# Maximum units in pairs on two row halves of TensorE, and the first expert of a second MoE ahead of its routing weights

## The reference

```python
# latent attention: 16 heads, 64 latent features, 1444 context positions a batch row
q_r = jnp.einsum('bshq,hqr->bhsr', q_big, W_qr)
k_r = jnp.einsum('bld,hdr->bhlr', kv_r, W_kr)
scores = jnp.einsum('bhsr,bhlr->bhsl', q_r, k_r)
attn = jax.nn.softmax(scores, axis=-1)
ctx_c = jnp.einsum('bhsl,bld->bhsd', attn, kv_r)
# second MoE: 32 experts, 8 of them a token, inner size 128, and a shared expert
router_scores = jax.nn.sigmoid(t @ Wr)
_, idx = jax.lax.top_k(router_scores + expert_bias[None, :], TOPK)
w = jnp.take_along_axis(router_scores, idx, axis=1)
w = w / jnp.sum(w, axis=-1, keepdims=True)
act = jax.nn.silu(g) * u
moe = jnp.einsum('tei,te,eih->th', act, wfull, Wd)
```

## Time and profile before

| what | us |
|---|---|
| median of 3 runs (1599.54 to 1603.27) | 1599.77 |
| the profiled execution's own time | 1590.53 |
| its span, first to last instruction | 1588.8 |
| PE busy / DVE / POOL / ACT | 1470.2 / 899.7 / 781.4 / 620.0 |
| latent attention: first to last reduction of a unit | 474.3 to 922.6 |
| first hidden product of the second MoE | 1359.69 |

### The profile page before, as it was taken

How to read it: one execution, slowest core, us unless ns; L and a number is a source line. 1 busy time by engine, 2 the same in 40 slices (tenths; PEclk the granted TensorE clock), 3 DMA queues, 4 the chain that set the end, 5 groups by cost and what they waited for, 6 DMA issues and landing times. The chain is left out here.

```text
span 1588.8 us, 20773 instructions
## 1 busy us (share of the span) xinstructions
PE 1470.2 (93%) x7316; PEld 1102.4 (69%) x7316; DVE 899.7 (57%) x1581; ACT 620.0 (39%) x1117; POOL 781.4 (49%) x605
## 2 busy tenths in 40 slices
PE   7898999899978999999999998978999998799998
PEld 4586565544445766766766665567988877799998
DVE  1573111255556676786776763567878774444444
ACT  2243121133341344344343342356666653333333
POOL 0760102135544897797797764057465541233332
PEclk7798999699997999999999999789999998899999
DMA  8004111611001010110110000200110001343441
GB/s 301 1 1 146 51 47 38 212 48 49 1 11 55 29 57 4 54 57 1 57 57 1 19 1 2 81 27 10 46 54 2 27 1 41 105 122 121 121 121 51
DMA packets 60317, 88.61 MB, mean 56 GB/s; under 512 B 7556, under 2 KB 44612, under 8 KB 60230
## 3 DMA queue, kind: packets, MB, share of 16 engines
q1 hardware_dynamic: 59206, 85.82, 16.9%
q0 software_dynamic: 1024, 1.64, 0.4%
HBM read 81.92 MB, written 5.41 MB: 55 GB/s over the span
## 5 line engine op out<-in xcount | busy, mean ns | idle before, releaser
L965 ACT ACTIVATE prob<-PS 121x800 f32<-121x800 f32 x192 | 158.3, 838 | 248.8 <-PE PS L1937 246.0
L1344 DVE TENSOR_REDUCE mx<-PS 128x1 f32<-128x482 f32 (+1 forms) x312 | 185.6, 649 | 44.7 <-PE PS L1917 43.5
L618 POOL TENSOR_TENSOR e_wl<-e_wf,e_wh 128x768 fp32r<-128x768 f32 x33 | 70.8, 2144 | 181.0 <-ACT e_wh L883 159.1
L695 POOL TENSOR_TENSOR hT<-hT,prob 121x800 f32<-121x800 f32 x56 | 109.3, 1951 | 66.4 <-ACT prob L965 64.3
L1916 PE MATMUL PS<-kth,qs 128*128 128x482 f32 (+1 forms) x312 | 128.6, 412 | 13.4 <-DVE kl L1337 5.8
L1952 PE MATMUL PS<-prob,kvn 121*64 121x400 f32 (+1 forms) x768 | 136.1, 503 | 0.9 <-ACT prob L965 0.9
L695 POOL TENSOR_TENSOR xc<-xc,prob 121x800 f32<-121x800 f32 x56 | 117.7, 2101 | 13.6 <-ACT prob L965 8.3
L1917 PE MATMUL PS<-kl,qm 66*128 66x482 f32 (+1 forms) x312 | 122.5, 393 | 0.0
L1934 PE MATMUL PS<-qs,kth 128*121 128x400 f32 (+1 forms) x384 | 111.6, 373 | 7.8 <-DMA qm<-nml 4.8
L1937 PE MATMUL PS<-qm,kl 66*121 66x400 f32 (+1 forms) x384 | 103.8, 352 | 0.0
L1952 PEld LDWEIGHTS PS<-prob,kvn 121*64 121x64 f32 (+1 forms) x768 | 52.3, 137 | 71.2 <-issue 68.6
(11 more groups left out here) (278 smaller groups left out, 3565.9 us busy)
## 6 DMA issues: line engine op xcount, KB each, us to landing
e_wb<-routing SPq DMA_DIRECT2D x32, 400.0 KB, 3.9
wgu<-in_L_ffn_gate_up_proj SPq DMA_DIRECT2D x8, 1024.0 KB, 14.0
krt<-in_ctx_T SPq DMA_DIRECT2D x8, 722.0 KB, 4.1
ksw<-in_ctx_Tswap SPq DMA_DIRECT2D x8, 722.0 KB, 5.7
wdn<-in_L_ffn_down_proj SPq DMA_DIRECT2D x8, 512.0 KB, 7.9
wq<-in_L_ffn_Wq SPq DMA_DIRECT2D x4, 1024.0 KB, 5.1
wo<-in_L_ffn_Wo SPq DMA_DIRECT2D x4, 1024.0 KB, 5.5
e_wf<-in_L_ffn_Wg SPq DMA_DIRECT2D x32, 128.0 KB, 2.2
```

What stands on the lines that cost most here:

```text
L618: pool.tensor_tensor(m["wl"][:, slot], m["wf"][:, slot], m["wh"][:, slot].bitcast(fp32), ALU.subtract).then_inc(ms["wlo"], 1)
L695: pool.tensor_tensor(acc, acc, prob[:, n % RING], ALU.add).then_inc(xb["ap"], 1)
L965: act.activation(prob[0:k, n % RING], PS[0:k, 2 * (n % 2):2 * (n % 2) + 2, 0:GC], ACT.Exp).then_inc(xb["ex"], 1)
L1344: dve.tensor_reduce(mx3[:, m, g:g + 1], PS[:, 4 + k % 3, 0:SEG[g][1]], AX.X, ALU.max).then_inc(xb["free"], 1)
```

## The change

In the latent attention a unit's second product has 64 rows. Units are issued in pairs: both high products, then both low ones, the first unit's on partitions 0 to 63 and the second's on 64 to 127, where `kl2` and `qm2` now have a second copy. The ones in rows 64 and 65 of `kl2` are written after a batch row's units, once per row; the scores keep their 66 rows. `UNITS` has mostly even steps, and in steps 8 and 14 the last two units are issued behind `values`. In the second MoE the barrier RT1 is gone, TensorE issues the first expert's hidden products ahead of the transposes of the routing weights, and the waits are moved to the places that need the data. The diff, cut to its core:

```diff
-        UNITS = (0, 0, 0, 0, 2, 4, 6, 8, 11, 14, 16, 18, 21, 24, 27, 30, 31, 33, 36, 39, 39, 39, 39, 39, 39)
+        UNITS = (0, 0, 0, 0, 2, 4, 6, 8, 10, 14, 16, 18, 20, 23, 25, 29, 31, 33, 36, 39, 39, 39, 39, 39, 39)
...
# GpSimd: keep[:] and its mask are gone; end_stage(ST_RT1) is gone on every engine
# ScalarE, high_queries
-                if b == 0:
-                    act.wait_ge(xb["z"], 3)
-                act.activation(qm2[:, b % 2], qs[0:DC + 2, b].rearrange("p h s -> p (h s)"), ACT.Copy,
-                               scale=keep[:, 0:1]).then_inc(xb["q2"], 1)
+                src = qs[0:DC, b].rearrange("p h s -> p (h s)")
+                act.activation(qm2[0:DC, b % 2], src, ACT.Copy).then_inc(xb["q2"], 1)
+                act.activation(qm2[DC:P, b % 2], src, ACT.Copy).then_inc(xb["q2"], 1)
...
# ScalarE, slices of the MoE; keep_routing copies the turned weights to rT2
                         gate(m, ms, n, k, first and k < 2)
+                        if first and k == 1:
+                            keep_routing()
...
-                            high_weights(m, ms, v + 1, (j + 1) % 4, turn0 + (j + 1) // 4 + 1, first and j < 3, each)
+                            high_weights(m, ms, v + 1, (j + 1) % 4, turn0 + (j + 1) // 4 + 1, first and j < 3, 48 if first and j == 0 else each)
...
# VectorE, product of the MoE
                     dve.wait_ge(ms["act"], n + 1)
+                    if first and k in (0, 2):
+                        dve.wait_ge(ms["ld"][k // 2], 64)
# VectorE, low_keys
-                dve.tensor_tensor(kl2[0:DC, b % 2, cols], krt[0:DC, cols], kth[0:DC, b % 2, cols].bitcast(fp32),
+                dve.tensor_tensor(kl2[:, b % 2, cols], krt[:, cols], kth[:, b % 2, cols].bitcast(fp32),
# VectorE, end of maxima_rows
+                dve.memset(kl2[DC:DC + 2, b % 2].bitcast(fp32), 1.0).then_inc(xb["one"], 1)
...
# TensorE, latent attention
+            def queries_keys(b, units):
+                banks = []
+                for u in units:
...
+                    banks.append(PS[:, next_slot((xb["free"], next(freed))), 0:SEG[g][1]])
+                    mm(banks[-1], qs[:, b].rearrange("p h s -> p (h s)")[:, cols], kth[:, b % 2, keys], start=True, stop=False)
+                for i, u in enumerate(units):
...
+                    rows = slice(DC * i, DC * i + DC)
+                    mm(banks[i], qm2[rows, b % 2, cols], kl2[rows, b % 2, keys], start=False, stop=True).then_inc(xb["fill"], 1)
+            def unit_pairs(b, first, end):
+                for u in range(first, end, 2):
+                    queries_keys(b, range(u, min(u + 2, end)))
...
# TensorE, in step s of the loop
-                        for u in range(UNITS[s], UNITS[s + 1]):
-                            queries_keys(b + 1, u)
+                        behind = 2 if s in (8, 14) else 0
+                        unit_pairs(b + 1, UNITS[s], UNITS[s + 1] - behind)
                     if s == 20 and more:
                         maxima_turned(b + 1)
                     if s % 6 == 2 and 8 <= n < B * SP_ + 3:
                         values((n - 8) // 6)
+                    if more and behind:
+                        unit_pairs(b + 1, UNITS[s + 1] - behind, UNITS[s + 1])
...
# TensorE, slices of the MoE
                         hidden(m, ms, n, k, j, va + j, q, first and k < 2)
+                        if first and k == 1:
+                            routing_turned()
+                            open_sums()
...
# TensorE, open_sums waits for the sigmoid and for both copies of the turned weights
+                pe.wait_ge(ro2["sig"], 1)
+                pe.wait_ge(ro2["te"], 2)
```

More of the change, by code:

```diff
@@ L195, in flamingo @@
         kth = sb("kth", [P, 2, SK], fp32r, stack=st3)
-        kl2 = sb("kl2", [DC + 2, 2, SK], fp32r, stack=st3)
-        qm2 = sb("qm2", [DC + 2, 2, HQ], fp32r, stack=st3)
+        kl2 = sb("kl2", [P, 2, SK], fp32r, stack=st3)
+        qm2 = sb("qm2", [P, 2, HQ], fp32r, stack=st3)
         prob = sb("prob", [KP, RING, 2, GC], stack=st3)
         ones = sb("ones", [KP, DC], stack=st3)
-        keep = sb("keep", [DC + 2, 1], stack=st3)
         mx3 = sb("mx3", [P, MT, 3], stack=st3)
@@ L522, in _ @@
                 load_routing(j, j)
-            end_stage(sp, ST_RT1)
             with sp.Fori(1, E1 // 4) as it:
@@ L1089, in _, with keep_routing @@
             act.wait_ge(ro2["lg"], 1)
[L1090 to L1094, removed]
+            act.activation(sc2[:], PS[0:S, 6, 0:B * E1].rearrange("p (b e) -> p b e", e=E1), ACT.Sigmoid).then_inc(ro2["sig"], 1)
+            def keep_routing():
+                for h in range(2):
+                    act.wait_ge(ro2["t"], h + 1)
+                    act.activation(rT2[:, half(h)], PS[0:E1, 4 + h, 0:HALF], ACT.Copy).then_inc(ro2["te"], 1)
             slices(moe1, ms1, 0, 4, True, 64, 0)
@@ L1397, in latent_residual @@
                 next(freed)
-            dve.memset(kl2[DC:DC + 2].bitcast(fp32), 1.0).then_inc(xb["one"], 1)
             for g in range(3):
@@ L1664, in _ @@
             end_stage(pe, ST_N1)
[L1666 to L1673, removed]
-                        last = pe.transpose(PS[0:E, 2 + h, j * S:(j + 1) * S], wt[:, h * HB + j, :], ident[0:S, 0:S])
-                    last.then_inc(ro["t"], 1)
             for b in range(B):
@@ L1930, in scores @@
                     pe.wait_ge(xb["qm"], 64 * (b + 1))
+                    pe.wait_ge(xb["one"], b + 1)
                 if n >= 2:
@@ L1936, in scores @@
                 for g in range(2):
-                    last = mm(PS[0:key_rows(t), 2 * (n % 2) + g, 0:GC], kl2[:, b % 2, keys],
-                              qm2[:, b % 2, (2 * hp + g) * GC:(2 * hp + g + 1) * GC], start=False, stop=True)
+                    last = mm(PS[0:key_rows(t), 2 * (n % 2) + g, 0:GC], kl2[0:DC + 2, b % 2, keys],
+                              qm2[0:DC + 2, b % 2, (2 * hp + g) * GC:(2 * hp + g + 1) * GC], start=False, stop=True)
                 last.then_inc(xb["s"], 1)
@@ L1958, in probability_sums @@
                 k = next_slot((xb["sums"], i + 1))
+                if i == 0:
+                    pe.wait_ge(xb["z"], 1)
                 pe.wait_ge(xb["ad"], 3 * i + 3)
@@ L1971, in project @@
                 last.then_inc(xb["fill"], 1)
-            for u in range(NU):
-                queries_keys(0, u)
+            unit_pairs(0, 0, NU)
             maxima_turned(0)
@@ L2099, in _, with routing_turned @@
             end_stage(pe, ST_R1)
-            route(ro2, h1, wr, E1, wn2)
-            end_stage(pe, ST_RT1)
+            for b in range(B):
+                for c in range(NC):
+                    last = mm(PS[0:S, 6, b * E1:(b + 1) * E1], h1[:, c, toks(b)], wr[:, c, :], start=(c == 0), stop=(c == NC - 1))
+            last.then_inc(ro2["lg"], 1)
+            def routing_turned():
+                pe.wait_ge(ro2["wt"], 1)
+                for h in range(2):
+                    for j in range(HB):
+                        last = pe.transpose(PS[0:E1, 4 + h, j * S:(j + 1) * S], wn2[:, h * HB + j, :], ident[0:S, 0:S])
+                    last.then_inc(ro2["t"], 1)
             pe.wait_ge(ms1["hl"], 1)
-            open_sums()
             slices(moe1, ms1, 0, 4, True)
```

32 lines of the change are left out of this document (10 added, 22 removed).

## The result

The changed kernel is slower: 1736.75 us in the median of 4 runs (1733.4 to 1741.6) against 1600.74 for the kernel before, a ratio of 1.0843, with a 95% interval of 1.0813 to 1.0873. The direction was forecast, the size was not: +136 us where +68 was forecast, above the range. The profiled execution took 1739.55 us.

The account below looks back on a forecast made before the run. TensorE was taken to bound the loop; 31.4 (shape changes) + 28 (block) + 9 (clock) - 4 (other waits) + 9 (first row) - 5.5 (MoE) = +68 us, so 1668 us, range 1608 to 1692 at 80%.

Parts of the forecast that it names:

- The price of a shape change: Attention loop, rows 1 to 7: switching TensorE between whole array and row halves costs 0.20 us each; term +31.4 us.
- the rival in which they run one after the other: A pair's two row-half low products don't overlap; 1698 us, chance 7%.
- The rival of a nearly free change: Changing array shape costs almost nothing, loop term -27 us; total 1586 to about 1605 us, chance 15%.
- The block behind step 8: VectorE's sums, context and addition work starts only after units 12 and 13; TensorE stands 5.0 us in six rows: +28 us.
- The rival that it costs little: The step 8 wait is absorbed and the clock holds; 1631 us, chance 17%.
- The term called the clock: Behind each of six step 8 waits, 3.4 us of work at half clock: +9 us, bounds 0 and 20.
- "At nothing": Query copy as two ScalarE instructions in step 2 costs nothing, lying under 4.2 us of value products; 11 us without cover.
- The first batch row: Its 39 units, in pairs, take 1.64 us a pair against 1.13 at full clock: +9 us, bounds 4 and 12.
- The other waits: TensorE's other waits for VectorE's reductions in the loop become fewer, from 14.7 us: -4 us, bounds 0 to -7.
- The MoE's start: Second MoE: first expert's hidden products start when the router's end: -5.5 us, bounds 0 and -6.5.

Follow-up runs that it names:

- single64: Kernel before with low (second) products of 64 rows, one unit at a time, no pairs, no units moved: 1722.1 us, ratio 1.0768.
- shape_changes: Kernel before plus one small overwritten product (64 rows, 64 columns) ahead of the first unit of 16 steps per batch row: 1643.0 us, ratio 1.0270.
- block_ahead: Changed kernel with VectorE's step 8 work (inverting sums, normalising context, adding probabilities) ahead of reducing units 12 and 13: 1674.0 us, ratio 1.0456 to before.
- both_mended: Changed kernel with VectorE's step 8 block ahead of reducing units 12 and 13, and query copies in steps 0 and 1: 1686.5 us, ratio 1.0531 to before.
- first_row_plain: both_mended, but the first batch row's units one by one with low products on 66 rows: 1659.9 us, ratio 1.0375 to the kernel before.
- filled: Changed kernel plus useless whole-array products, 10 ahead of unit 3 and 25 ahead of unit 17, from batch row 1 on: 1683.6 us, ratio 1.0515 to before.
- pairs_full: Kernel before with the MoE part, pairs and new UNITS, but low products on all 66 rows and one query copy: 1665.2 us, ratio 1.0386.
- second_copy: Kernel before with ScalarE's query copy done twice in step 2, the second time the same values: 1611.9 us, ratio 1.0056.
- whole_array_tuned: Kernel before with the MoE part, query copy in step 0, and one unit instead of two in step 10: 1608.8 us, ratio 1.0060.

## Why the prediction came out too low

**The price of a shape change held, its term came out too large.** 0.20 us a change was taken. Where the clock is full, low products start 0.31 behind the high ones, scores 0.41 behind the low ones, and single64 and shape_changes give 0.16 to 0.17 in the mean. Row halves do run together, which no row of before had shown; the rival in which they run one after the other fell. The rival of a nearly free change fell too. But where a whole batch row with the pairs lies at the full clock (one row of block_ahead, one of both_mended, two of first_row_plain), TensorE is busy 62.6 to 62.9 us, against 59.5 to 59.9 in such rows before: about 3.1 more, not 4.5, and some 22 us in seven rows, not 31.4. A small part of the difference lies at the value products: the way to them from the last low product grew by 0.10 us only (0.41, before 0.31), not by 0.20. The rest is not explained.

**The block behind step 8 held**, place and size: 5.12 to 5.14 us between starts, six times, by the mechanism given. The rival that it costs little fell.

**The term called the clock failed**, and this is the step that makes most of the error. It put 3.4 us at the lower level behind each wait and 9 us in all. Its basis was one wait of 1.3 us in the kernel before, in work without shape changes, and it was carried over to waits of 5 us in work with many. Measured are stretches of 17.1 to 20.5 us behind the waits of 5 us. The kernel before had better rows for this. It waits 4.75 us once, for the first row's maxima, and lies at the lower clock from 498.2 to 518.7, 15.8 us of that behind the wait. And behind waits of 1.78 and 1.53 us, longer than the one used, its clock doesn't fall at all. Windows of the kernel before on the first, and the product behind the 1.78:

```profile
498.00:503.00 5.00, 0.24 (x2) 0.52 0.02 3
503.00:519.00 16.00, 14.20 (x40) 0.51 0.33 117
713.76:720.00 6.24, 6.24 (x30) 1.00 0.00 1
```
```profile
713.76 0.49 PE L1916 MATMUL PS<-kth,qs 128*128 128x482 f32 x1 [1.78 <-DVE mx L1344]
```

An estimate from that row: 16 us at the lower clock behind each of six waits, 14.2 of them busy, would have lost some 43 us, not 9.

What the low stretches cost in the loop is the difference of the changed kernel to filled, 60.7 us, or a little more, since the filler takes up to 1 us a row longer than the waits that it fills. The rest of the loop's +130.8 is TensorE's idle time, +40.7, and the shape changes, some +22: 123 to 130 in all. The terms of the prediction, 31.4 + 28 - 4, and 13 for the waits of step 4 make 68.4, close to the 70.1 that filled has over before. That is luck: the shapes are 10 too high in the sum, the idle time is 4 too low, and the 70.1 has what the filler takes over the waits in it.

Two parts of the mechanism are shown. An idle TensorE brings the clock down: filled fills the waits, block_ahead takes the long ones away, and in both the lower stretches behind them go. And the work behind decides how soon it comes back: at waits of the same length, 4.7 to 4.9 us, in the same step, the clock is low for 6.8 to 10.2 us with the low products on the whole array (pairs_full) and for 17.1 to 20.5 with row halves. With row halves a wait of 1.4 us in that step can bring as much (block_ahead), while one of 2.1 us in step 4 brings 6.8, 10.2, 13.7 or nothing. What in this work delays it stays open, the changes of shape or the products of 64 rows themselves; no run separates the two.

**"At nothing" failed for the query copy**: some 13 us of waits (six of 2.1) and their clock in the changed kernel, 8 us alone in second_copy. The prediction named the scores of step 5 as what would be late; late was the chain from high keys over low keys to reductions.

**The first batch row was mis-sized**: +9 forecast, +19.7 measured, and for another reason than the sum has. The work lost to the lower clock there (half of the time TensorE is busy at it) is 22.1 us against 3.2, nearly the whole difference. What pairs would cost in this row at the full clock stays open, since no run had them at it.

**The other waits** (-4) had nothing to shrink. The 14.7 us that the term starts from are idle time of the weight loads; the products themselves waited 5.4 us, 4.6 of them in the three waits of the blocks. Instead the waits for VectorE's sums grew from 1.7 to 6.2 us. **The MoE's start** held: -5.9 for -5.5.

The chances were given to mechanisms that differ in the shape change and the block, which were both right. None was given to the clock, which had bounds of 0 and 20 us from a single row. (The free-change rival with the other terms as taken is 1600 - 27 + 36.5 = 1609 us, not 1605; nothing hangs on it.)

## What to carry to other kernels

Where TensorE is the bound, a wait costs more than its length: here 5 us of waiting cost up to 10 us more in clock behind it (17.1 to 20.5 us at half speed), so the order of a helper engine's queue is worth as much as the products. That price can't be taken from one short wait in other work: look through the whole trace for a wait of the expected length, and at what runs behind it. And an instruction added on an engine that is a third busy is free only if nothing behind it in its own queue, nor in the queue that this feeds, is due.

## What was unexpected of the hardware

- Useless products made the kernel faster: 245 of them, -53 us.
- Alternating products of 128 and 64 rows left a low clock low for 102 us, though in a window of it TensorE was busy 54.4 of 55.0 us. In the loop the same alternation ran at the full clock without losing it (single64).
- Pairs on the whole array also kept it low through the first row, 38.5 us with 37.4 busy, where single units raised it.
- Three low keys of VectorE, 64x482 each, took 5.97 us beside a working GpSimd (whole_array_tuned), some 4.3 beside one in the kernel before, and 1.79 there ahead of the first row, where GpSimd had nothing to do.
